# Batch attention of a fused perceiver block: gate and power projections laid between the halves of scores and values, cosine products on VectorE

## The chip, the cores and the metric

The kernel runs on one NeuronCore of one Trainium2 chip. The metric is the device time of one execution in microseconds (us), the median of several runs. Of the core's engines the text names TensorE (PE in the rows, PEld for its weight loads), VectorE (DVE), ScalarE (ACT), GpSimd (POOL) and SyncE (SP), which only issues DMAs here.

## The reference, cut to what matters

The reference is six residual sublayers over x of 32 x 32 tokens by 512. The change lies in the second one. It is an attention over the 32 sequences of each time step's batch, with 16 heads of 32, where keys and queries are scaled by two running quantities, a gate and a power:

```python
q = _l2norm((xn @ Wq).reshape(Bx, Tx, H, Dh))
k = _l2norm((xn @ Wk).reshape(Bx, Tx, H, Dh))
v = (xn @ Wv).reshape(Bx, Tx, H, Dh)
clock = jax.nn.softplus(xn @ clock_w + clock_b).reshape(Bx, Tx, H, 1)
q = _rope(q, times)                      # pairs turned by cos and sin of the token's place
k = _rope(k, times)
gj = -jax.nn.softplus(xn @ gate_w + gate_b).reshape(Bx, Tx, H, Dh)
gcp = jnp.exp(jnp.clip(jnp.cumsum(gj, axis=1), -60.0, 50.0))
q = q * gcp
k = k / (gcp + 1e-08)
p = (xn @ p_w + p_b).reshape(Bx, Tx, H, Dh)
p_max = jnp.max(p, axis=1, keepdims=True)
p_exp = jnp.exp(p - p_max) * clock
p_cs = jnp.cumsum(p_exp, axis=1)
q = q / (p_cs + 1e-08)
k = k * p_exp
scores = jnp.einsum('bqhd,bkhd->bhqk', q, k) / math.sqrt(Dh)
scores = jnp.where(mask[None, None], scores, -jnp.inf)
attn = jax.nn.softmax(scores, axis=-1)
out = jnp.einsum('bhqk,bkhd->bqhd', attn, v).reshape(Bx, Tx, D)
```

The other sublayers (a delayed-aggregation attention before it; a GELU MLP, a mixture of small experts, a cross attention, a state-space scan and a ternary MLP behind it) are not touched.

## The kernel before

All activations are held transposed: 128 features on the partitions, 1024 token columns, four feature groups `o` = 0 to 3 of four heads each. A projection of one group onto one half of the tokens is one **unit**: `project_half` (L506 is its matmul, inside `linear`) multiplies four 128x128 blocks of a weight with four 128x512 blocks of XN into one PSUM bank. All is fp32, and the trace shows each fp32 matmul as two rows, so a unit is 8 rows of L506. The weights are bq, bk (queries, keys), bg (gate), bp (power) and bv (values).

PSUM has eight banks in two rings of four. A bank of the first ring is filled by TensorE and emptied by ScalarE (`open_act`, semaphores act_bank_full and act_bank_free); one of the second is emptied by VectorE (`open_dve`). A ring's bank number u can be opened when number u-4 has been emptied, so the order of the units in a ring must be the same on both engines. Every engine's order is written out by hand; nothing is planned by a program.

For one group o the steps are these. ScalarE takes the gate's projection out of PSUM with its bias (`gate_half`, L1285) and makes log(1+exp) of it with three activations (`gates_in`, L1299 to L1301). It takes out the power's projection (`powers_in`, L1318) and makes two exponentials (`gates_exp`, L1322 and L1324). VectorE does the running sums and the quotient (`gates`, L1854 to L1876, among them a RECIPROCAL of 128x1024 at L1871). TensorE spreads the clock (`clocks`, L630), projects queries and keys, turns them by a matrix (`rotations`, L638) and sums squares (`norm_sums`, L648), while ScalarE copies and squares them (`queries_keys`, L1330, L1196). VectorE multiplies the turned ones by sin (`rotate`, L1882), and GpSimd multiplies the plain ones by cos (L2386); VectorE adds and scales (L1887 to L1890) and makes the norm's inverse (`norm`, L1895, L1896). TensorE spreads it (`norm_spread`, L659), and VectorE multiplies it in (`spread_norm`, L1902). Then `scores` lays the causal mask (L670) and multiplies queries and keys in 128 tiny matmuls of 32x32 (L680, 256 rows), ScalarE takes exp (L1357), `values` multiplies with the values in another 128 tiny matmuls (L694, 256 rows), VectorE divides (`normalise`, L1909, L1910), and `turn` transposes (L704).

The loop over o on TensorE runs: bp of group o+1, clocks(o+1), scores(o), turn(o-1), bq and bk of o+1, rotations(o+1), norm_sums(o+1), bg of group o+2 (for o below 2), values(o), norm_spread(o+1). VectorE's loop is gates(o+1), rotate(o+1), norm(o+1), normalise(o), spread_norm(o+1).

The arena has six slots of 1 MB for weights. `free_after_act` and `free_after_dve` note at which count of a ring's full banks a slot may be loaded again; SyncE waits for that count. Behind the loop the first weight of the MLP goes into the slot of bk and the second into that of bg.

Of the kernel before, what the change touches and what calls it, by code (L numbers as in the profile page):

```python
# [17 lines left out]
C2 = N // 512  # L18
# [76 lines left out]
def perceiver(nc, dram, out):  # L95
# [6 lines left out]
    with ctx:  # L102
# [364 lines left out]
        def _(pe):  # L467
# [195 lines left out]

            def scores(o):

                heads = [open_act(("s", o, h)) for h in range(4)]
                for i in range(4):
                    for h in range(4):
                        hp = slice(32 * h, 32 * h + 32)
                        mm(heads[h][32 * i:32 * i + 32, 0:256].rearrange("p (x n) -> p x n", x=TT), tab("ident")[hp, hp],  # L670
                           tab("causal")[hp, :].unsqueeze(1).to_broadcast([32, TT, 32]), start=True, stop=False,
                           tile_position=(32 * h, 32 * i), skip_group_check=True)
                for tt in range(TT):
                    if tt % 4 == 0:
                        on_dve(("n", o, 1, tt // 4))
                    for i in range(4):
                        tok = slice(128 * tt + 32 * i, 128 * tt + 32 * i + 32)
                        for h in range(4):
                            hp = slice(32 * h, 32 * h + 32)
                            last = mm(heads[h][32 * i:32 * i + 32, 32 * tt:32 * tt + 32], H[hp, 0, 1, tok], H[hp, 0, 0, tok],  # L680
                                      start=False, stop=(tt == TT - 1), tile_position=(32 * h, 32 * i), skip_group_check=True)
                            if tt == TT - 1 and i == 3:
                                last.then_inc(act_bank_full, 1)

            def values(o):
                for u in range(4):
                    on_act(("s", o, 3))
# [33 lines left out]
            for c in range(C2):  # L721
                features(0, c, "plain")
            norm_spread(0)
            for o in range(4):
                if o < 3:
                    project(o + 1, ("bp",))
                    clocks(o + 1)
                scores(o)
                if o:
# [5 lines left out]
                if o < 2:  # L735
                    project(o + 2, ("bg",))
# [3 lines left out]
            for w in ("bq", "bk", "bg", "bp"):  # L740
                free_after_act(w)
            turn(3)
# [443 lines left out]
        def _(act):  # L1186
# [118 lines left out]
            def gates_in(o):  # L1305

                if o:
                    for c in range(C2):
                        gate_half(o, c)
                act.wait_ge(act_bank_free, UA.at[("bg", o, C2 - 1)] + 1)  # L1310
# [35 lines left out]
            for c in range(C2):  # L1346
                features(0, c, Y, "plain")
            for o in range(4):
                if o < 3:
                    powers_in(o + 1)  # L1350
# [11 lines left out]
                if o < 2:  # L1362
                    gates_in(o + 2)
            turned(3)
# [304 lines left out]
        def _(dve):  # L1669
# [179 lines left out]
            def gates(o):  # L1849
# [13 lines left out]
                for c in range(C2):  # L1863
                    b = unit(("ck", o, c))
                    v.tensor_tensor(p[:, ch(c)], b[:, :], p[:, ch(c)], ALU.mult).then_inc(dve_bank_free, 1)
                stored(("ck", o, C2 - 1))
# [11 lines left out]
            def rotate(o):  # L1878
                for w, t_ in (("bq", t0), ("bk", t1)):
                    for c in range(C2):  # L1880
# [3 lines left out]
                                        tab("sin").unsqueeze(1).to_broadcast([128, 16, L]), ALU.mult).then_inc(dve_bank_free, 1)  # L1884
                stored(("rbk", o, C2 - 1))
# [488 lines left out]
        def _(pool):  # L2374
# [6 lines left out]
            for o in range(4):  # L2381
                for i, w in enumerate(("bq", "bk")):
                    pool.wait_ge(act_bank_free, UA.at[(w, o, C2 - 1)] + 1)
                    pool.wait_ge(dve_bank_full, UV.at[("r" + w, o, C2 - 1)] + 1)
                    x3 = H[:, 0, i, :].rearrange("p (b l) -> p b l", l=L)
                    g.tensor_tensor(x3, x3, tab("cos").unsqueeze(1).to_broadcast([128, B, L]), ALU.mult).then_inc(S["b_cos"], 1)  # L2386
# [253 lines left out]
```

## Time and profile before

| what | value |
| --- | --- |
| median of 3 runs | 2265.08 us (2259.3 to 2266.7) |
| the profiled execution, its own time | 2268.11 us |
| its span in the trace | 2266.3 us |
| mean granted TensorE clock | 0.974 of full |
| TensorE busy (matmul) | 2110.3 us, 93% |
| VectorE busy | 1249.2 us, 55% |
| ScalarE busy | 921.0 us, 41% |
| GpSimd busy | 91.3 us, 4% |

Times in the rows are us from the start of the span unless marked ns. A row of the timeline gives the start, the busy time, engine, line, operation, output and input, the shape, how many instructions are merged, and in brackets how long the engine stood idle before and what ended that. "issue" as the ender means that the profile shows nothing that the engine waited for. The granted clock is 1.00 at TensorE's upper level (2.4 GHz) and 0.50 at its lower (1.2 GHz). The batch attention's loop lies between 248 and 430 us.

### The profile page before, as it was taken

The numbers are of one execution on the slowest core, as the hardware profiler recorded it, in microseconds if no ns is written. First come the engines' busy times: TensorE is split into PE (matmuls) and PEld (weight loads), VectorE is DVE, ScalarE is ACT, GpSimd is POOL, SyncE is SP. The second block draws the span as 40 slices with busy tenths as digits, with TensorE's granted clock in tenths as the row PEclk, the third lists the DMA queues.
The fourth block names the chain that finished last, engine by engine and source line by source line (L and its number), as shares of the span: only waits on it lengthen the run. The fifth ranks groups of instructions, "written<-read, shape, count | busy, mean of one in ns | idle before, by whom it ended". The sixth has DMA issues, their size and how long they took to land. (4 is left out here: it accounts for less than half of the span.)

```text
span 2266.3 us, 35893 instructions
## 1 busy us (share of the span) xinstructions
PE 2110.3 (93%) x14950; PEld 1533.4 (68%) x14950; DVE 1249.2 (55%) x2086; ACT 921.0 (41%) x2211; POOL 91.3 (4%) x119
## 2 busy tenths in 40 slices
PE   6999898689999999989998999999999999988899
PEld 5764444468867888844445788778878778774587
DVE  4255466363345888799998310544354443456563
ACT  3224333053424323599996332232232322323432
POOL 0000011000000000100000000000000000000122
PEclk9999988799999999999999999999999999999999
DMA  6120000111210110120002144322121121232000
GB/s 237 34 86 1 1 2 2 39 56 38 75 43 19 38 56 22 54 93 19 1 1 94 42 162 145 103 63 65 43 85 43 55 73 43 67 113 91 1 1 37
DMA packets 84872, 127.01 MB, mean 56 GB/s; under 512 B 6998, under 2 KB 48470, under 8 KB 84248
## 3 DMA queue, kind: packets, MB, share of 16 engines
q1 hardware_dynamic: 84712, 124.73, 16.6%
q8 instruction: 119, 1.95, 0.4%
q14 instruction: 41, 0.34, 0.0%
HBM read 109.77 MB, written 14.94 MB: 55 GB/s over the span
## 5 line engine op out<-in xcount | busy, mean ns | idle before, releaser
L1196 ACT ACTIVATE R<-bank 128x512 f32<-128x512 f32 (+3 forms) x157 | 93.0, 597 | 466.8 <-PE bank L891 335.6
L1426 ACT ACTIVATE R<-R 128x64 f32<-128x64 f32 x1024 | 248.0, 356 | 0.0
L891 PE MATMUL bank<-cth,wmh 128*128 128x512 f32 x512 | 208.0, 406 | 7.1 <-ACT arena L1527 6.9
L891 PE MATMUL bank<-cth,wml 128*128 128x512 f32 x512 | 202.3, 395 | 0.0
L891 PE MATMUL bank<-ctl,wmh 128*128 128x512 f32 x512 | 202.0, 395 | 0.0
L506 PE MATMUL bank<-XN,arena 128*128 128x512 f32 x320 | 153.1, 635 | 0.5 <-ACT R L1357 0.5
L891 PEld LDWEIGHTS bank<-cth,wmh 128*128 128x128 f32 x512 | 96.3, 188 | 35.3 <-issue 16.1
L506 PE MATMUL bank<-Y,arena 128*128 128x512 f32 x256 | 117.6, 605 | 0.0
L506 PEld LDWEIGHTS bank<-XN,arena 128*128 128x128 f32 x320 | 64.0, 205 | 78.6 <-issue 77.8
L2173 DVE COPY Y<-bank 128x512 f32<-128x512 f32 x128 | 79.5, 683 | 61.6 <-PE bank L929 61.5
L891 PEld LDWEIGHTS bank<-cth,wml 128*128 128x128 f32 x512 | 96.2, 188 | 22.1
L891 PEld LDWEIGHTS bank<-ctl,wmh 128*128 128x128 f32 x512 | 96.4, 188 | 20.0
L764 PE MATMUL bank<-hid_high,piece_high 128*128 128x512 f32 x256 | 100.3, 392 | 6.2 <-DVE hid_low L2089 6.2
L1527 ACT ACTIVATE arena<-bank,small 128x289 f32<-128x289 f32 x128 | 62.5, 501 | 99.6 <-PE bank L940 52.4
L764 PE MATMUL bank<-y_high,piece_high 128*128 128x512 f32 x256 | 99.8, 390 | 0.0
L764 PE MATMUL bank<-hid_high,piece_low 128*128 128x512 f32 x256 | 99.7, 390 | 0.0
L764 PE MATMUL bank<-y_high,piece_low 128*128 128x512 f32 x256 | 99.7, 390 | 0.0
L764 PE MATMUL bank<-hid_low,piece_high 128*128 128x512 f32 x256 | 99.7, 390 | 0.0
L764 PE MATMUL bank<-y_low,piece_high 128*128 128x512 f32 x256 | 99.7, 389 | 0.0
L2160 DVE TENSOR_TENSOR ctl<-H,cth 128x2048 fp32r<-128x2048 f32 x15 | 34.4, 2293 | 103.4 <-ACT cth L1502 103.4
L1234 ACT ACTIVATE piece_high<-arena 128x512 fp32r<-128x512 f32 x80 | 48.8, 624 | 102.4 <-PE bank L764 102.1
L506 PEld LDWEIGHTS bank<-Y,arena 128*128 128x128 f32 x256 | 49.5, 195 | 60.3 <-issue 60.0
(418 smaller groups left out, 4429.3 us busy)
## 6 DMA issues: line engine op xcount, KB each, us to landing
H<-in_ctxT SPq DMA_DIRECT2D x30, 512.0 KB, 5.1
arena<-in_L_attn_mlp_w SPq DMA_DIRECT2D x8, 1024.0 KB, 5.2
arena<-spill SPq DMA_DIRECT2D x32, 256.0 KB, 5.4
spill<-R SPq DMA_DIRECT2D x3, 2048.0 KB, 8.3
spill<-XN SPq DMA_DIRECT2D x3, 2048.0 KB, 8.3
arena<-in_L_ffn_Wg SPq DMA_DIRECT2D x4, 1024.0 KB, 7.1
arena<-in_L_ffn_Wu SPq DMA_DIRECT2D x4, 1024.0 KB, 5.2
arena<-in_L_ffn_Wd SPq DMA_DIRECT2D x4, 1024.0 KB, 5.5
```

Of the source, the lines that this page charges most:

```text
L506: last = mm(bank, w[:, k, cols_], x[:, k, xc], start=(k == 0), stop=(k == 3 and not more))
L764: last = mm(b[:, :], w_, x_[:, k, ch(c)], start=(k == 0 and i == 0), stop=(k == 3 and i == 2))
L891: last = mm(b[:, :].rearrange("p (a c) -> p a c", a=2), w_, c_[:, k, :, :], start=(k == 0 and n_ == 0), stop=(k == 3 and n_ == 2))
L1196: fn(dst, src, ACT.Copy).then_inc(act_bank_free, 1)
L1234: fn(piece_high[:, n % PIECES], W(name)[:, :, tl(o)], ACT.Copy).then_inc(S["w_high"], 1)
L1426: last = fn(EE[n % 3][:, a:a + 64], RC["Ey"][:, t, h, :], ACT.Copy, scale=RC["Ex"][:, t, h, 8 * j + x:8 * j + x + 1])
L1527: fn(RDa["p"][:, g, 320 * (bb % 2):320 * (bb % 2) + 289], b[:, 0:289], ACT.Exp, bias=small[:, 16 + x:17 + x], scale=HD1 ** -0.5, accum_out ...
L2160: v.tensor_tensor(ctl[:, :, :, :], ct if pr else ct_first, cth[:, :, :, :].bitcast(f32), ALU.subtract).then_inc(S["d_clo"], 1)
L2173: v.tensor_copy(RD["vt"][:, 2 * (bb % 2) + blk, 512 * half:512 * half + 512], b[:, :]).then_inc(dve_bank_free, 1)
```

## The change

On TensorE the gate's projections of groups 2 and 3 (two units each) leave their place ahead of values(o) and go into the scores of group o: the first unit after half of the tiny matmuls, the second right after the last. They are now written into VectorE's ring of banks. The power's projections of groups 2 and 3 leave the head of the loop and go into values(o), before its third and fourth quarter; group 1's two go ahead of the loop, before norm_spread(0). VectorE takes the gate's projections of groups 2 and 3 out of PSUM, with the bias, in the middle of gates(o+1); ScalarE no longer does. ScalarE's powers_in moves behind gates_in. The products with cos go from GpSimd to VectorE, inside rotate. The slot of bg is released by the count of VectorE's ring.

```diff
--- before.py
+++ after.py
@@ -661,6 +661,10 @@
                             if s_ == 3:
                                 last.then_inc(dve_bank_full, 1)
 
+            def gate_unit(o, c):
+                b = open_dve(("bg", o, c))
+                linear(b[:, :], W("bg"), tl(o), XN, ch(c)).then_inc(dve_bank_full, 1)
+
             def scores(o):
 
                 heads = [open_act(("s", o, h)) for h in range(4)]
@@ -671,6 +675,8 @@
                            tab("causal")[hp, :].unsqueeze(1).to_broadcast([32, TT, 32]), start=True, stop=False,
                            tile_position=(32 * h, 32 * i), skip_group_check=True)
                 for tt in range(TT):
+                    if tt == 4 and o < 2:
+                        gate_unit(o + 2, 0)
                     if tt % 4 == 0:
                         on_dve(("n", o, 1, tt // 4))
                     for i in range(4):
@@ -684,6 +690,8 @@
 
             def values(o):
                 for u in range(4):
+                    if u in (2, 3) and o < 2:
+                        project_half("bp", o + 2, u - 2)
                     on_act(("s", o, 3))
                     b = open_dve(("pv", o, u))
                     for t in range(2):
@@ -720,25 +728,26 @@
             pe.wait_ge(S["n_plain"], TT)
             for c in range(C2):
                 features(0, c, "plain")
+            project(1, ("bp",))
             norm_spread(0)
             for o in range(4):
                 if o < 3:
-                    project(o + 1, ("bp",))
                     clocks(o + 1)
                 scores(o)
+                if o < 2:
+                    gate_unit(o + 2, 1)
                 if o:
                     turn(o - 1)
                 if o < 3:
                     project(o + 1, ("bq", "bk"))
                     rotations(o + 1)
                     norm_sums(o + 1)
-                if o < 2:
-                    project(o + 2, ("bg",))
                 values(o)
                 if o < 3:
                     norm_spread(o + 1)
-            for w in ("bq", "bk", "bg", "bp"):
+            for w in ("bq", "bk", "bp"):
                 free_after_act(w)
+            free_after_dve("bg")
             turn(3)
             weight("bo")
             on_act(("turn", 3, 1))
@@ -1304,10 +1313,13 @@
 
             def gates_in(o):
 
-                if o:
+                if o == 1:
                     for c in range(C2):
                         gate_half(o, c)
-                act.wait_ge(act_bank_free, UA.at[("bg", o, C2 - 1)] + 1)
+                if o < 2:
+                    act.wait_ge(act_bank_free, UA.at[("bg", o, C2 - 1)] + 1)
+                else:
+                    vrow(("bg", o, C2 - 1))
                 if o:
                     act.wait_ge(S["b_gcs"], o)
                 log1pexp(gate_buf[o % 2], RB["lg"][:, 0, :], S["b_gsp"])
@@ -1345,9 +1357,9 @@
             gates_in(1)
             for c in range(C2):
                 features(0, c, Y, "plain")
+            powers_in(1)
             for o in range(4):
                 if o < 3:
-                    powers_in(o + 1)
                     gates_exp(o + 1)
 
 
@@ -1361,6 +1373,7 @@
                     queries_keys(o + 1)
                 if o < 2:
                     gates_in(o + 2)
+                    powers_in(o + 2)
             turned(3)
 
             def inputs(c):
@@ -1863,6 +1876,10 @@
                 for c in range(C2):
                     b = unit(("ck", o, c))
                     v.tensor_tensor(p[:, ch(c)], b[:, :], p[:, ch(c)], ALU.mult).then_inc(dve_bank_free, 1)
+                if 0 < o < 3:
+                    for c in range(C2):
+                        v.tensor_scalar(gate_buf[(o + 1) % 2][:, ch(c)], unit(("bg", o + 1, c))[:, :], col("L0_attn_gate_b", o + 1), None, ALU.add
+                                        ).then_inc(dve_bank_free, 1)
                 stored(("ck", o, C2 - 1))
                 step(v.tensor_tensor_scan(pcs, reset[:, 0, :], p, 0.0, ALU.mult, ALU.add))
                 step(v.tensor_scalar(pcs, pcs, 1e-8, None, ALU.add))
@@ -1876,12 +1893,16 @@
                 step(v.tensor_tensor(rg, g, rg, ALU.mult))
 
             def rotate(o):
-                for w, t_ in (("bq", t0), ("bk", t1)):
+                cos = tab("cos").unsqueeze(1).to_broadcast([128, B, L])
+                for w, t_, x in (("bq", t0, q), ("bk", t1, k)):
                     for c in range(C2):
                         b = unit(("r" + w, o, c))
                         v.tensor_tensor(t_[:, ch(c)].rearrange("p (b l) -> p b l", **byb),
                                         b[:, :].rearrange("p (b l) -> p b l", **byb),
                                         tab("sin").unsqueeze(1).to_broadcast([128, 16, L]), ALU.mult).then_inc(dve_bank_free, 1)
+                    on_act((w, o, C2 - 1))
+                    x3 = x.rearrange("p (b l) -> p b l", **byb)
+                    v.tensor_tensor(x3, x3, cos, ALU.mult).then_inc(S["b_cos"], 1)
                 stored(("rbk", o, C2 - 1))
                 dve.wait_ge(S["b_cos"], 2 * (o + 1))
                 v.tensor_tensor(q, q, t0, ALU.add)
@@ -2378,12 +2399,6 @@
             g.memset(RA["m"], 0.0).then_inc(m_zero, 1)
             pool.wait_ge(in_consts, 32)
             end_stage()
-            for o in range(4):
-                for i, w in enumerate(("bq", "bk")):
-                    pool.wait_ge(act_bank_free, UA.at[(w, o, C2 - 1)] + 1)
-                    pool.wait_ge(dve_bank_full, UV.at[("r" + w, o, C2 - 1)] + 1)
-                    x3 = H[:, 0, i, :].rearrange("p (b l) -> p b l", l=L)
-                    g.tensor_tensor(x3, x3, tab("cos").unsqueeze(1).to_broadcast([128, B, L]), ALU.mult).then_inc(S["b_cos"], 1)
             end_stage()
             end_stage()
             pool.wait_ge(dve_bank_full, UV.at[("cu", NQ - 1, 3, C2 - 1)] + 1)
```

## Rows read from the trace of the kernel before

**Rows 1.** Page: busy time by engine, clock by slice, instruction queue (packets, MB, share)
```profile
PE 2110.3 (93%) x14950; PEld 1533.4 (68%) x14950; DVE 1249.2 (55%) x2086; ACT 921.0 (41%) x2211; POOL 91.3 (4%) x119
PEclk9999988799999999999999999999999999999999
q8 instruction: 119, 1.95, 0.4%
```

**Rows 2.** TensorE's timeline, group 0, from the spread of the norm to its scores
```profile
248.42 1.72 PE L659 MATMUL bank<-H,consts 32*128 32x128 f32 x32
250.07 7.13 PE L506 MATMUL bank<-XN,arena 128*128 128x512 f32 x16
257.13 1.98 PE L630 MATMUL bank<-R,consts 16*128 16x512 f32 x4
259.04 0.72 PE L670 MATMUL bank<-consts 32*32 32x256 f32 x32
...
261.61 1.29 PE L680 MATMUL bank<-H 32*32 32x32 f32 x128 [0.78 <-issue]
265.06 0.36 PE L680 MATMUL bank<-H 32*32 32x32 f32 x16 [2.17 <-issue]
265.90 16.99 PE L506 MATMUL bank<-XN,arena 128*128 128x512 f32 x32 [0.47 <-ACT R L1357]
```

**Rows 3.** TensorE's timeline, from group 0's values to the start of group 3
```profile
294.32 2.55 PE L694 MATMUL bank<-R 32*32 32x33 f32 x256
...
299.03 1.69 PE L659 MATMUL bank<-H,consts 32*128 32x128 f32 x14 [0.67 <-issue]
300.65 9.81 PE L506 MATMUL bank<-XN,arena 128*128 128x512 f32 x16
...
312.30 0.71 PE L670 MATMUL bank<-consts 32*32 32x256 f32 x32
...
352.12 0.56 PE L694 MATMUL bank<-R 32*32 32x33 f32 x40 [2.12 <-issue]
...
366.92 0.71 PE L670 MATMUL bank<-consts 32*32 32x256 f32 x32
...
390.58 3.60 PE L638 MATMUL bank<-H,consts 128*128 128x512 f32 x8
...
404.63 3.22 PE L659 MATMUL bank<-H,consts 32*128 32x128 f32 x32 [4.58 <-DVE R L1910]
```

**Rows 4.** Stretches: length, busy PE, PEld, DVE, ACT, POOL, clock, DMA, GB/s
```profile
252.01:301.76 49.75, 45.67 (x683) 23.61 (x682) 36.78 (x39) 19.09 (x26) 4.66 (x2) 0.91 0.01 2
266.00:268.00 2.00, 2.00 (x3) 0.97 (x4) 1.97 (x2) 0.67 (x3) 0.00 (x0) 0.50 0.04 8
272.00:274.00 2.00, 2.00 (x6) 0.94 (x5) 1.97 (x2) 1.08 (x2) 0.00 (x0) 1.00 0.00 0
299.00:299.50 0.50, 0.47 (x7) 0.47 (x8) 0.29 (x1) 0.50 (x1) 0.00 (x0) 0.75 0.00 0
```

**Rows 5.** Timelines of ScalarE, VectorE and GpSimd, gates and rotation of groups 1 and 2
```profile
260.47 1.06 ACT L1324 ACTIVATE R<-R 128x1024 f32<-128x1024 f32 x1 [0.18 <-DVE R L1860]
267.20 6.55 DVE L1871 RECIPROCAL R<-R 128x1024 f32<-128x1024 f32 x1
284.75 4.66 POOL L2386 TENSOR_TENSOR H<-H,consts 128x1024 f32<-128x1024 f32 x2 [79.29 <-PE bank L638]
289.51 1.23 DVE L1887 TENSOR_TENSOR H<-H,R 128x1024 f32<-128x1024 f32 x1 [2.47 <-POOL H L2386]
311.22 1.22 DVE L1859 TENSOR_REDUCE R<-H 128x32 f32<-128x1024 f32 x1 [5.19 <-ACT H L1318]
```

**Rows 6.** The loop's end: TensorE, SyncE's issues, a stretch (columns of rows 4)
```profile
425.38 0.66 PE L694 MATMUL bank<-R 32*32 32x33 f32 x32 [5.29 <-issue]
415.45 1.64 SPq L2439 DMA_DIRECT2D arena<-in_L_attn_mlp_w  x2
418.00:420.00 2.00, 1.88 (x127) 1.85 (x127) 0.88 (x4) 0.00 (x0) 0.00 (x0) 0.50 1.12 377
```

## The prediction, made before the changed kernel ran

> **What bounds the kernel now.** I read the page first: TensorE is busy 93% of the span, and its granted clock, near full nearly everywhere, dips in slices 5 to 7, that is from 283 to 453 us [rows 1]. The batch attention lies there. Then I read TensorE's timeline through its loop. A group takes 53.3 us at first (mask row at 259.04 to mask row at 312.30) and 54.6 us then (to 366.92) [rows 2, 3], and the reader should see that three things in it are no work.
>
> First, waits with the ender "issue" inside the runs of tiny matmuls: 0.78 and 2.17 us in group 0's scores, 0.67 us behind its values, 2.12 us in group 1's values [rows 2, 3]. A tiny matmul goes by in some 10 ns (128 rows in 1.29 us), and the waits come 128 rows apart [rows 2]. With their weight loads these are 256 instructions, and the instruction queue moved 1.95 MB in 119 packets, 16.4 KB each, 64 bytes for each of 256 instructions [rows 1]. I read the waits as instruction blocks that are used up before the next is there. From the end of one wait (261.61) to the end of the next (265.06) are 3.45 us [rows 2]; I take that as the pace at which blocks come. A unit of a projection is 8 rows and takes 7.13 / 2 = 3.57 us [rows 2]: 16 instructions in which the queue catches up by a whole block.
>
> Second, the clock. At 266 it is at its lower level, where 32 rows of bq and bk take 16.99 us against 2 x 7.13 = 14.3, so 2.7 us are lost; at 272 it is back at the upper [rows 2, 4]. It falls again near 299.2, and bp of group 2 takes 9.81 us against 7.13, again 2.7 lost [rows 3, 4]. Before the first fall TensorE had done nothing full-width since bp and clocks ended at 259.1, before the second nothing since 294.3: only tiny matmuls and waits. Third, 0.47 us of wait for ScalarE's exp [rows 2].
>
> VectorE is not behind: of the 49.75 us between the starts of two gates it is busy 36.78 [rows 4], and it waits for the power's projection (5.19 us in group 2) [rows 5]. Its chain becomes important below.
>
> **TensorE in groups 0 and 1.** No matmul is added or removed. Group 0 without the three losses is 53.3 - (0.78 + 2.17 + 0.67) - 0.47 - 2.7 - 2.7 = 43.8 us. *The waits for instructions.* With a unit after half of the scores' tiny matmuls, another behind them and two between the quarters of values, nearly any 256 instructions in a row contain a unit or the clocks' 1.98 us [rows 2], so the pace of 3.45 us is kept. Between 0 and 2.2 us (one whole wait) may stay for each group, depending on where block ends lie; I take 0. *The wait for exp:* the second gate unit, 3.57 us, lies between the last score and bq, and exp of four banks is over by then; 0 stays.
>
> *The clock.* The values' stretch is cut into pieces below 2.3 us between units, and I drop its fall. But with bp gone from the loop's head, the stretch from values' last unit to the scores' first unit holds only narrow work: last quarter 0.6, norm_spread 1.7, clocks 1.98, mask and half the scores 2.1, and handovers, 6.4 to 7.4 us. The two falls came 4.9 us (294.3 to 299.2) and at most 7 us (259.1 to 266) after the last wide work [rows 2 to 4]. So I keep one fall for each group, which now slows the gate units in the scores. Its price is 0 (none) to 2.7 us; I take 1.8, since part of a low stretch lies on tiny matmuls that are bound otherwise. Group 0 then takes 45.6 us, a gain of 7.7. Group 1 has the same work and one turn, 8 rows of a quarter of a unit's columns, 3.57 / 4 = 0.9 us: 46.5 us, and 54.6 - 46.5 = 8.1.
>
> **VectorE in groups 0 and 1.** It gets two PSUM reads of 128x512 for the gate. No row has this form; half of an L1887 row (1.23 us for 128x1024) is 0.62, a whole one 1.23 [rows 5]; I take 0.7 each, nearer to the row of its width, 1.4 in all (1.2 to 2.5). It gets two cos products with L1887's shape, 2 x 1.23 = 2.5 us. Against that goes its wait for GpSimd, which needed 4.66 us for the pair, 2.47 of it shown as VectorE's wait [rows 5]: on VectorE the first product falls into gaps between the rotations, and the last ends about 0.4 us earlier than GpSimd's. In group 0's own rotation the 2.5 us are hidden by the value projection and by the features behind it. The chain from one gates to the next is 36.78 + 1.4 + 2.5 = 40.7 us, plus 1.1 for ScalarE's exponential of the power [rows 5], plus about 1 for handing the norm to TensorE and back: 42.8 us. The 5.19 us wait goes, since bp is out of PSUM before VectorE asks. So VectorE runs just below TensorE's 43.8 to 46. **The added wait:** VectorE now waits for the second gate unit in the middle of gates. Behind it stand the scan, the RECIPROCAL of 6.55 us [rows 5], rotate and norm, and norm_spread waits for them. I get the unit done 0.4 to 0.8 us after VectorE is ready; that fits in the slack and is not charged.
>
> **Ahead of the loop.** bp of group 1 was behind norm_spread(0) and covered its reading by VectorE; now it stands before. TensorE's sum is the same, scores(0) start some 0.3 us later (bank handovers). VectorE's first gates start 7 us later, at 259, which the chain above contains. Cost 0.3.
>
> **Group 2.** Here the cover is gone: bp and clocks stood ahead of scores(2), now only clocks. VectorE starts gates(3) about when scores(2) start. ScalarE makes the two exponentials of the gate and power first: before, from 252.01 to 260.47 + 1.06, 9.5 us, less 1.7 us of waiting for bp, 7.8 us [rows 4, 5]. Scores take 3.5 us and a wait of about 1.8, so TensorE stands about 2.5 us until exp of the scores frees a bank for turn. Behind it is bq and bk. From the rotations (390.58) to norm_spread (404.63, 4.58 us late) [rows 3] VectorE's chain decides, and it is 0.4 us shorter. Net -2.1 (0 to -5).
>
> **The loop's end.** Two MLP weights of 1 MB each start at 415.45 and fill the DMA engines (share 1.12 at 418 to 420), and TensorE then waits 5.29 us for instructions [rows 6]. bg's slot is now released by VectorE's ring, whose count at that place includes the last values bank. So the second MB starts only when values(3) is over, where wide matmuls follow and the next stage still is far. Other waits of this kind are up to 2.2 us, so the gain lies between 0 and 3.1; I take 2.5. SyncE has nothing else queued behind.
>
> **Sum.** 7.7 + 8.1 - 0.3 - 2.1 + 2.5 = 15.9 us. Against the profiled execution's 2268.11 us that is 2252.2; the median of the runs, 2265.08, lies 3.0 below that execution, so the forecast is 2249.2 us.
>
> **A rule against it.** The rows above show 0.78 + 2.17 + 0.67 + 2.12 = 5.7 us of "issue" in two groups [rows 2, 3] and one packet for each 256 instructions [rows 1]. The Trainium skill, "Runtime: NRT & Kernel Launch", section "Instruction fetch mechanics", has the same 16 KiB blocks, but gives TensorE a store of 128 KiB, eight blocks, and calls the crossing of a block mostly hidden; a run of some 580 instructions could then never wait. By that rule the waits have another cause and would stay: that is the first rival. The waits 128 rows apart speak against it.
>
> **Rivals.** *The waits and falls stay* (the tiny matmuls themselves are the cause). Then only the exp wait (1), the weight's delay (2.5) and VectorE's lost wait for bp count, less 2.4: about 3 to 6 us, 2260.5. For it: I infer the blocks. Against: their regular distance. Chance 0.12. *VectorE becomes the bound:* its reads cost 1.23 us each, and with each late gate unit (a fall stretches the unit to 7 us) the whole chain moves, 3 us more for each group: gain 10, 2255.1. For it: 42.8 stands only 1 us below 43.8. Chance 0.17. *No fall at all:* 2 x 1.8 more, and the first MB hurts less: gain 20.5, 2244.6. For it: every stretch of narrow work gets shorter in total. Chance 0.2. *Slower:* with a unit between runs of tiny matmuls the clock stays down: in the rows it came back within bq and bk, a row of 16.99 us of nothing but wide work [rows 2, 4]. All wide work of groups 0 and 1, about 8 units and the rotations, 32 us each, runs at half speed: each group loses up to 32 us instead of 1.8. It becomes slower than before when the loss is over 15.9 / 2 + 1.8 = 10 us for each group, about 20 us of wide work at the low level; if half of the wide work ran so, 2 x 14 more, 2277. Against it: bq, bk and the rotations are still 18 us in a row. Chance 0.03.
>
> **How the numbers follow.** The forecast's case has 0.48. Its own bounds (a wait of 2.2 left in each group, a fall at 2.7, no gain at the end) reach 2257; the best case reaches 2244.6, and the before runs themselves spread by 7 us. Range 2240 to 2258. A change below 0.3%, 6.8 us, can't be told from none here. Faster: 0.48 + 0.17 + 0.2 and a quarter of the first rival, 0.88; same 0.08; slower 0.04.
>
> **What would show it.** Right: "issue" waits inside L680 and L694 of groups 0 and 1 gone; mask rows 45 to 47 us apart; bq and bk back at 14.3 us; at most one stretch at 0.50 for each group, lying on the gate units; ScalarE's wait for bp gone; one 1 MB load before and one after values(3). Wrong: VectorE's wait at its second gate read above 2 us, norm_spread waiting for L1910 in groups 1 and 2 by more than 2 us, or the waits moved to other rows.

## The result, and the profile after

| | median | runs | range |
| --- | --- | --- | --- |
| before | 2265.4 us | 5 | 2259.3 to 2266.7 |
| changed | 2248.23 us | 5 | 2244.97 to 2251.45 |

The ratio is 0.9924, with a 95% interval of 0.9908 to 0.994. That is 17.2 us faster by the medians; the forecast was 15.9 us, 2249.2. The profiled execution of the changed kernel took 2248.23 us, its span is 2246.2.

TensorE's timeline of group 0 and the start of group 1 (start, busy time, instruction, and in brackets the idle time before and what ended it) answers [rows 2] and the start of [rows 3]. L674, L686 and L702 are now the mask, the scores and the values:

```profile
255.38 1.72 PE L659 MATMUL bank<-H,consts 32*128 32x128 f32 x32
257.40 1.95 PE L630 MATMUL bank<-R,consts 16*128 16x512 f32 x4 [0.31 <-DVE H L1923]
259.28 0.71 PE L674 MATMUL bank<-consts 32*32 32x256 f32 x32
259.74 1.33 PE L686 MATMUL bank<-H 32*32 32x32 f32 x112
261.52 0.29 PE L686 MATMUL bank<-H 32*32 32x32 f32 x16 [0.44 <-issue]
261.74 3.70 PE L506 MATMUL bank<-XN,arena 128*128 128x512 f32 x8
265.37 1.29 PE L686 MATMUL bank<-H 32*32 32x32 f32 x128
266.59 17.43 PE L506 MATMUL bank<-XN,arena 128*128 128x512 f32 x40
...
288.40 1.35 PE L702 MATMUL bank<-R 32*32 32x33 f32 x128
289.68 3.70 PE L506 MATMUL bank<-XN,arena 128*128 128x512 f32 x8
...
302.77 1.15 PE L674 MATMUL bank<-consts 32*32 32x256 f32 x32
```

The reader is to see three things. Of the waits for instructions, 0.78 and 2.17 us in the scores and 0.67 us behind the values, 0.44 us in the scores is left. A unit of 8 rows stands behind 128 tiny rows. And the 40 rows from 266.59 (the second gate unit, bq and bk) take 17.43 us, where 32 rows took 16.99 before [rows 2]: the clock is at its upper level. Group 0 takes 43.5 us (259.28 to 302.77), where it took 53.3.

Group 1's scores, first before and then changed:

```profile
314.90 1.27 PE L680 MATMUL bank<-H 32*32 32x32 f32 x128 [1.24 <-issue]
318.63 0.91 PE L680 MATMUL bank<-H 32*32 32x32 f32 x67 [2.46 <-issue]
```

```profile
303.62 1.77 PE L686 MATMUL bank<-H 32*32 32x32 f32 x128
305.32 4.12 PE L506 MATMUL bank<-XN,arena 128*128 128x512 f32 x8
```

The prediction counted 5.7 us of "issue" in the two groups; with these two waits, which it left out, they are 9.4 us. All 5.8 us of group 1's are gone. Group 1 takes 44.3 us (302.77 to 347.11), where it took 54.6.

From group 2 on, the same view answers the end of [rows 3] and the first row of [rows 6]:

```profile
347.11 1.16 PE L674 MATMUL bank<-consts 32*32 32x256 f32 x32
...
350.67 1.53 PE L686 MATMUL bank<-H 32*32 32x32 f32 x127 [0.96 <-issue]
354.94 2.08 PE L712 MATMUL bank<-consts,R 128*128 128x128 f32 x8 [2.74 <-ACT R L1369]
356.81 15.89 PE L506 MATMUL bank<-XN,arena 128*128 128x512 f32 x32
...
385.96 3.22 PE L659 MATMUL bank<-H,consts 32*128 32x128 f32 x32 [3.75 <-DVE R L1931]
...
394.42 0.32 PE L686 MATMUL bank<-H 32*32 32x32 f32 x22 [1.81 <-issue]
...
404.13 0.67 PE L702 MATMUL bank<-R 32*32 32x33 f32 x32 [3.96 <-issue]
...
408.29 17.11 PE L506 MATMUL bank<-R,arena 128*128 128x512 f32 x35 [0.73 <-issue]
```

The 2.74 us ahead of turn are the new wait for exp that the missing cover gives. The last wait for instructions fell from 5.29 to 3.96 us. The first bo row starts at 408.29 instead of 429.54.

VectorE's timeline of group 1 and a stretch of all engines (length, busy PE, PEld, DVE, ACT, POOL, clock, DMA share, GB/s) answer [rows 4, 5]:

```profile
267.94 0.74 DVE L1881 TENSOR_SCALAR H<-bank,cols 128x512 f32<-128x512 f32 x1
270.33 0.75 DVE L1881 TENSOR_SCALAR H<-bank,cols 128x512 f32<-128x512 f32 x1 [1.64 <-PE bank L506]
...
288.00 1.21 DVE L1905 TENSOR_TENSOR H<-H,consts 128x1024 f32<-128x1024 f32 x1
```

```profile
258.97:302.45 43.48, 42.53 (x685) 22.03 (x684) 39.86 (x42) 17.44 (x24) 0.00 (x0) 1.00 0.01 2
302.00:304.00 2.00, 2.00 (x50) 0.77 (x52) 1.97 (x3) 0.00 (x0) 0.00 (x0) 0.70 0.00 0
304.00:306.00 2.00, 2.00 (x128) 1.75 (x126) 1.99 (x1) 0.00 (x0) 0.00 (x0) 0.50 0.04 8
306.00:308.00 2.00, 2.00 (x6) 0.77 (x5) 1.94 (x3) 1.06 (x1) 0.00 (x0) 0.95 0.00 0
```

Between the starts of two gates VectorE is now busy 39.86 of 43.48 us, TensorE 42.53: both are nearly full. The gate's read costs 0.74 us, the cos product 1.21. The second read waits 1.64 us for its unit. In this execution group 0 has no low stretch of the clock at all; one lies between 302 and 306, on clocks, mask and scores of group 1.

Since whole executions of one kernel differ by 7 us and more, the experiments are read by stretches of the loop as well: the group lengths are from mask row to mask row, the end from norm_spread(3) to the first bo row, the loop from group 0's mask row to the first bo row. Each line of the table is from one profile, also that of before, whose execution was 2.7 us above its median (2268.1 against 2265.4); the gain is that of the medians, against the runs of before on the same chip.

| kernel | group 0 | group 1 | mask(2) to norm_spread(3) | end | loop | median | gain |
| --- | --- | --- | --- | --- | --- | --- | --- |
| before | 53.3 | 54.6 | 37.7 | 24.9 | 170.5 | 2265.4 | |
| changed | 43.5 | 44.3 | 38.9 | 22.3 | 149.0 | 2248.2 | 17.2 |
| e1 nothing laid between | 50.2 | 52.7 | 38.0 | 23.2 | 164.2 | 2261.5 | 4.9 |
| e2 scores whole | 47.8 | 48.3 | 37.8 | 23.0 | 156.8 | 2254.0 | 12.4 |
| e3 values whole | 48.1 | 49.8 | 36.5 | 22.8 | 157.2 | 2258.6 | 7.8 |
| e4 cos on GpSimd | 45.0 | 43.5 | 39.0 | 22.8 | 150.3 | 2246.4 | 19.9 |
| e5 both loads early | 45.0 | 44.4 | 37.8 | 25.2 | 152.4 | 2252.0 | 15.6 |
| e6 both loads late | 45.4 | 43.6 | 38.2 | 20.8 | 148.0 | 2251.2 | 16.4 |
| e7 e6 and exp first | 47.3 | 44.3 | 36.8 | 21.1 | 149.5 | 2251.6 | 16.0 |
| e8 filler | 45.2 | 45.1 | 37.6 | 24.4 | 152.2 | 2252.0 | 15.6 |
| e9 changed, again | 47.0 | 44.5 | 39.0 | 23.0 | 153.4 | 2247.6 | 19.2 |
| e10 combined | 45.0 | 44.3 | 39.3 | 21.7 | 150.3 | 2249.4 | 17.4 |

### The profile page after: what moved, and what is told of

The parts are those of the page before. It is cut to its first block and busy times, and to the rows that moved or that the text cites. A ratio compares the mean times of both kernels' runs of the same rounds, so it can differ in the third digit from the quotient of the medians.

```text
span 2246.2 us, 35885 instructions
## 1 busy us (share of the span) xinstructions
PE 2102.9 (94%) x14950; PEld 1528.6 (68%) x14950; DVE 1258.8 (56%) x2098; ACT 917.9 (41%) x2207; POOL 72.6 (3%) x111
## 3 DMA queue, kind: packets, MB, share of 16 engines
q8 instruction: 119, 1.95, 0.4%
## 5 line engine op out<-in xcount | busy, mean ns | idle before, releaser
L506 PE MATMUL bank<-XN,arena 128*128 128x512 f32 x320 | 146.4, 610 | 0.0
L900 PEld LDWEIGHTS bank<-cth,wml 128*128 128x128 f32 x512 | 96.2, 188 | 22.3
L900 PEld LDWEIGHTS bank<-ctl,wmh 128*128 128x128 f32 x512 | 96.5, 188 | 20.1
L1243 ACT ACTIVATE piece_high<-arena 128x512 fp32r<-128x512 f32 x80 | 48.8, 624 | 102.9 <-PE bank L773 102.7
```

The costliest lines, as they stand in the source:

```text
L506: last = mm(bank, w[:, k, cols_], x[:, k, xc], start=(k == 0), stop=(k == 3 and not more))
L900: last = mm(b[:, :].rearrange("p (a c) -> p a c", a=2), w_, c_[:, k, :, :], start=(k == 0 and n_ == 0), stop=(k == 3 and n_ == 2))
L1243: fn(piece_high[:, n % PIECES], W(name)[:, :, tl(o)], ACT.Copy).then_inc(S["w_high"], 1)
```

## The experiments

### e1: the same order, nothing laid between

```diff
-                    if tt == 4 and o < 2:
-                        gate_unit(o + 2, 0)
...
-                    if u in (2, 3) and o < 2:
-                        project_half("bp", o + 2, u - 2)
...
                 scores(o)
                 if o < 2:
+                    gate_unit(o + 2, 0)
                     gate_unit(o + 2, 1)
...
+                if o < 2:
+                    project(o + 2, ("bp",))
                 values(o)
```

> The changed kernel with its four gate units behind the whole scores and its four power units ahead of the whole values, so no unit lies between tiny matmuls; all else as changed (the power of group 1 ahead of the loop, gate read and cos on VectorE, late weight slot). If the laying between pays (blocks of instructions arrive every 3.45 us and the clock holds when wide work comes between), the waits for instructions come back: about 2 to 3.5 us in each of the scores of groups 0 and 1, 0.7 to 2 us in each of their values, and each group shows a low clock on the units behind; groups 0 and 1 take some 50 us instead of 43.5 and 44.3, and the kernel is 9 to 13 us slower than the changed one, about 2259. If the gain came from the order alone (VectorE's wait for the power's projection gone), they stay at 43.5 to 45 us and the time at 2248 to 2250.

Measured: 2261.49 us, ratio to before 0.9982 (0.9967 to 0.9996); groups 0 and 1 take 50.2 and 52.7 us. TensorE's timeline of group 1 and the end of group 0 in e1:

```profile
305.73 1.60 PE L659 MATMUL bank<-H,consts 32*128 32x128 f32 x29 [0.90 <-issue]
...
316.36 0.77 PE L684 MATMUL bank<-H 32*32 32x32 f32 x67 [2.19 <-issue]
317.06 8.83 PE L506 MATMUL bank<-XN,arena 128*128 128x512 f32 x16
...
356.14 0.99 PE L698 MATMUL bank<-R 32*32 32x33 f32 x56 [2.13 <-issue]
```

The waits are back, 2.2 us in scores and 2.1 in values, and two gate units take 8.83 instead of 7.13 us: a low clock. All the rest of the change gives 6.3 us of the loop (170.5 less 164.2); the laying between gives 15.2 by the changed kernel's first profile (149.0), 10.8 by its second (153.4, e9), and 12.3 by the medians (17.2 less 4.9). The expectation held in kind. The time, told as 9 to 13 us over the changed kernel and about 2259, came out 13.3 over it and at 2261.5.

### e2 and e3: one of the two laid between

e2 is the scores' part of e1's edit alone, e3 the values' part alone:

```diff
e2:
-                    if tt == 4 and o < 2:
-                        gate_unit(o + 2, 0)
...
                 if o < 2:
+                    gate_unit(o + 2, 0)
                     gate_unit(o + 2, 1)
e3:
-                    if u in (2, 3) and o < 2:
-                        project_half("bp", o + 2, u - 2)
...
+                if o < 2:
+                    project(o + 2, ("bp",))
                 values(o)
```

> The changed kernel with only the gate units taken out of the scores and put behind them. If block supply bounds the tiny matmuls: waits of 1.5 to 3.5 us in the scores of each of groups 0 and 1, then a low clock on the gate units; groups 0 and 1 each 3 to 5 us longer, kernel 2254 to 2258. The second gate unit then ends that much later, and VectorE's wait at its second read grows by the same amount from the 1.64 and 2.16 us it has. If the waits are due to something else, nothing appears and the time stays near 2248.

> The changed kernel with only the power units taken out of the values and put ahead of them. The values then run as 256 rows on end: a wait of 0.7 to 2.1 us for instructions in each of groups 0 and 1 and a longer narrow stretch to the scores of the next group (values, norm_spread, clocks, half the scores: some 8 to 9 us), on which the clock falls in both groups; 1.5 to 4 us more for each group, kernel 2251 to 2256. If VectorE's chain decides the group's length, the waits hide behind its norm and only the clock's part shows: under 2 us in all.

e2: 2253.95 us, 0.9954 (0.9936 to 0.9972); the loop is 7.8 us longer than the changed kernel's. e3: 2258.59 us, 0.9966 (0.9953 to 0.9979); 8.2 us longer. These are against the first profile. Groups 0 and 1 together took 87.8 to 91.6 us, mean 89.7, in the eight profiles that have them as changed (e9 below); e2 takes 96.1 (6.4 more), e3 97.9 (8.2 more), e1 102.9 (13.3 more). The two sum to 14.6, so the parts are near additive. From e2, group 1's scores, then from e3, group 1's values and what follows:

```profile
310.69 0.91 PE L684 MATMUL bank<-H 32*32 32x32 f32 x67 [2.00 <-issue]
311.53 8.75 PE L506 MATMUL bank<-XN,arena 128*128 128x512 f32 x16
```

```profile
347.70 0.84 PE L700 MATMUL bank<-R 32*32 32x33 f32 x56 [1.90 <-issue]
348.48 3.10 PE L659 MATMUL bank<-H,consts 32*128 32x128 f32 x32
351.42 3.75 PE L630 MATMUL bank<-R,consts 16*128 16x512 f32 x4
```

In e2 a wait of 2.00 us and 1.6 us of low clock on the two units behind. In e3 a wait of 1.90 us, then norm_spread and clocks at half speed: 3.10 and 3.75 us against 2.09 and 1.95. The expectation for e2 held (groups 4.3 and 4.0 us longer, 2254); VectorE's wait for the gate grew as told, but at both reads: 3.13 and 2.68 us in group 0, where the changed kernel's profile has none and 1.64. The one for e3 missed: 2258.6 us against 2251 to 2256, groups 4.6 and 5.5 us longer against 1.5 to 4. My bound for e3, that VectorE's chain might hide it, falls. By the gains (12.4 and 7.8 us) e3 is the dearer of the two, but their intervals overlap. Waits for instructions make 2.7 us of e3's 8.2 in groups 0 and 1 (0.83 and 1.90); most of the rest is narrow work at the lower clock, as in the rows above. In group 2 e3 wins 2.4 us back: TensorE waits 0.89 us for exp and 0.70 for instructions at turn instead of 2.74 for exp, and bq and bk take 14.53 us instead of 15.89; its wait for VectorE's side ahead of norm_spread(3) is no shorter (4.22 against 3.75).

### e8: a unit in scores(3) that computes nothing needed

```diff
+                    if tt == 4 and o == 3:
+                        b = open_dve("filler")
+                        linear(b[:, :], W("bp"), tl(0), XN, ch(0)).then_inc(dve_bank_full, 1)
...
+                if o == 2:
+                    v.tensor_copy(small[:, 40:48], unit("filler")[:, 0:8]).then_inc(dve_bank_free, 1)
```

> The changed kernel with one more unit, whose product is thrown away, after half of the tiny matmuls of scores(3). If blocks of instructions come every 3.45 us, the unit's 3.57 us give the time for the next: the 1.81 us wait in those scores goes wholly, and the price of the added unit (3.5 us at the upper level, up to 7 at the lower) is partly paid: net 1.7 to 5 us slower. If the wait belongs to the tiny matmuls, it stays at 1.8 and the kernel is 3.5 us or more slower.

TensorE's timeline through the scores of group 3 in e8 (L689 are the scores, L715 is turn):

```profile
388.28 1.16 PE L674 MATMUL bank<-consts 32*32 32x256 f32 x32
389.13 1.76 PE L689 MATMUL bank<-H 32*32 32x32 f32 x128
390.82 4.67 PE L506 MATMUL bank<-XN,arena 128*128 128x512 f32 x8
395.42 1.29 PE L689 MATMUL bank<-H 32*32 32x32 f32 x128
397.23 1.06 PE L715 MATMUL bank<-consts,R 128*128 128x128 f32 x8 [0.52 <-ACT R L1372]
```

The wait of 1.81 us in these scores is gone. Nothing else in them changed, so it was no property of the tiny matmuls: it goes when 4.67 us of other work stand in their middle. From mask to turn it takes 8.95 us against 6.22 (389.11 to 395.33 in the changed kernel) and 6.58 (e9), so a unit of 4.67 us costs 2.4 to 2.7 there, and 1.4 to 2.1 over the whole end (24.4 us against 22.3 and 23.0), around the low end of the 1.7 to 5 expected. The median, 2252.02 us (0.9927, 0.991 to 0.9944), can't tell that from the changed kernel.

### e5 and e6: when the MLP's weights are loaded

e5 releases bg's slot by ScalarE's ring again; e6 releases bk's slot by VectorE's too:

```diff
e5:
-            for w in ("bq", "bk", "bp"):
+            for w in ("bq", "bk", "bg", "bp"):
                 free_after_act(w)
-            free_after_dve("bg")
e6:
-            for w in ("bq", "bk", "bp"):
+            for w in ("bq", "bp"):
                 free_after_act(w)
-            free_after_dve("bg")
+            for w in ("bk", "bg"):
+                free_after_dve(w)
```

> The changed kernel with the slot of bg released by ScalarE's ring again, so that both 1 MB weights start together as before the change. My step for the loop's end: the second MB in front of TensorE's instruction block makes its last wait in values(3) about as long as before, 5.3 us, instead of the 3.96 us that it has now: 1.3 to 2.5 us slower, norm_spread(3) to the first bo row 23.6 to 24.9 us instead of 22.3. Rival: the wait is set by the first MB alone; then it stays near 4 us and nothing changes.

> The changed kernel with the slot of bk released by VectorE's ring too, so both weights start only when values(3) is over. If the DMAs in front of the instruction block make part of the 3.96 us wait, it falls to the 1.8 to 2.2 us that the other waits have, and the kernel gets 1.8 to 2.2 us faster, about 2246; the weights still arrive more than 20 us before the next stage. If the wait is no matter of the DMA queue, it stays 3.96 us and the time with it.

The last wait in values(3), e5 and then e6:

```profile
408.67 0.67 PE L702 MATMUL bank<-R 32*32 32x33 f32 x32 [5.58 <-issue]
```

```profile
404.81 0.67 PE L702 MATMUL bank<-R 32*32 32x33 f32 x32 [1.45 <-issue]
```

With 2 MB in front the wait is 5.58 us (5.29 before). With 1 MB it is 3.96, and 2.82 to 4.32 in the seven profiles that have this. With none it is 1.45 in e6 and e7, 2.60 in e10. The end takes 25.2, 22.3 and 20.8 us in e5, changed and e6. The instruction queue's own packets separate the cases better: the packet ahead of this wait started behind the one before it by 7.3 and 7.4 us with 2 MB, 5.2 to 5.8 with 1 MB, 3.4 to 4.0 with none. So the second MB adds 2 us; the rival, that the first MB alone sets the wait, is out.

The waits moved the way both expectations told, e6's further (1.45 us against 1.8 to 2.2). e5's end lies just over the 23.6 to 24.9 us told, and e6's time does not come out at 2246. The medians, 2252.03 (0.9931, 0.9915 to 0.9948) and 2251.18 us (0.9928, 0.991 to 0.9947), don't separate these few us; only the stretch shows them.

### e4: cos on GpSimd

```diff
-                    on_act((w, o, C2 - 1))
-                    x3 = x.rearrange("p (b l) -> p b l", **byb)
-                    v.tensor_tensor(x3, x3, cos, ALU.mult).then_inc(S["b_cos"], 1)
...
+            for o in range(4):
+                for i, w in enumerate(("bq", "bk")):
+                    pool.wait_ge(act_bank_free, UA.at[(w, o, C2 - 1)] + 1)
+                    pool.wait_ge(dve_bank_full, UV.at[("r" + w, o, C2 - 1)] + 1)
+                    x3 = H[:, 0, i, :].rearrange("p (b l) -> p b l", l=L)
+                    g.tensor_tensor(x3, x3, tab("cos").unsqueeze(1).to_broadcast([128, B, L]), ALU.mult).then_inc(S["b_cos"], 1)
```

> The changed kernel with the two cos products of each group back on GpSimd. My working: VectorE loses 2.4 us of work for each group but waits about 2.5 us for GpSimd's 4.66 us pair, which can start only when the last rotation is in. In groups 0 and 1 VectorE comes to the rotations late (at 286.8, the rotations done at 287.4), so GpSimd's pair, 287.5 to 292.2, lies in the open: VectorE's add starts at about 292.2 instead of 291.65, norm_spread some 0.5 us later in each group, and 0.4 us later in group 2; together 1 to 2 us slower, which a median can hardly tell. Rival: VectorE is the bound and its 2.4 us count fully: 2 us faster for each of groups 0 and 1, 4 to 5 us in all.

VectorE and GpSimd in e4, group 1's rotation:

```profile
286.84 2.48 DVE L1899 TENSOR_TENSOR R<-bank,consts 128x512 f32<-128x512 f32 x4
291.45 1.23 DVE L1904 TENSOR_TENSOR H<-H,R 128x1024 f32<-128x1024 f32 x1 [2.12 <-POOL H L2403]
```

```profile
285.92 5.42 POOL L2403 TENSOR_TENSOR H<-H,consts 128x1024 f32<-128x1024 f32 x2 [82.96 <-PE bank L638]
```

VectorE's add starts 4.61 us behind the start of its sin products, and in the changed kernel 4.86 (286.79 to 291.65). So in groups 0 and 1 moving cos to VectorE neither gains nor loses: 2.4 us of work replace 2.1 us of waiting. GpSimd begins with queries as soon as their rotation is in, which I had overlooked, and ends earlier than I said. 2246.41 us, 0.9925 (0.9899 to 0.9951). The 1 to 2 us slower and the rival's 4 to 5 us faster both lie within what the medians leave open; in the stretches neither is there (groups 0 and 1 take 88.5 us, of 87.8 to 91.6 in the eight).

### e9, e7 and e10: how far one profile can be trusted, and a try at more

e9 is the changed kernel, unchanged. e7 is e6 with the exps of scores(2) ahead of the power's exponential. e10 is e7 with turn(1) ahead of clocks(3):

```diff
                 fn(gate_buf[o % 2], RB["t"][:, 1, :], ACT.Exp).then_inc(S["b_gcp"], 1)
+                if o == 3:
+                    score_exps(2)
                 act.wait_ge(S["b_pdif"], o + 1)
...
+                if o == 2:
+                    turn(1)
                 if o < 3:
                     clocks(o + 1)
                 scores(o)
...
-                if o:
+                if o in (1, 3):
                     turn(o - 1)
```

> The changed kernel itself once more, on the same chip as the next one. In five runs above, all with groups 0 and 1 ordered as here, group 0 took 45.0 to 47.3 us where the changed kernel's profile has 43.5, each with a low stretch of the clock on the first gate unit (4.9 to 5.5 us instead of 3.7). If that profile was a lucky one, this one shows such a stretch in group 0 and 45 us or more; if the changed kernel is free of it by its own order, 43.5 us again. Time 2246 to 2252.

> The last one, and in group 2 ScalarE makes the four exps of the scores before the exponential of the power. TensorE's 2.74 us wait for them ahead of turn(1) falls to about 0.5 us; the power's exponential comes at most 0.3 us later, so VectorE, which had 2.0 us to spare at the rotations of group 3, becomes about level with TensorE. Group 2 up to norm_spread(3) gets 1.5 to 2.2 us shorter: 2244. If VectorE's chain already set group 2's end, under 0.5 us.

> The changed kernel with both MLP weights loaded behind values(3), the exps of scores(2) ahead of the power's exponential on ScalarE, and turn(1) ahead of clocks(3) instead of behind scores(2). Turn no longer stands between the scores' end and bq, and TensorE waits about 0.5 us there instead of 2.7: from the mask row of group 2 to its bq row 5.5 to 6.5 us instead of 9.7, then VectorE's chain (2.0 us to spare) takes back about half. Loop's end 1.5 us shorter as in the run with both loads late. In all 2.5 to 4.5 us faster than the changed kernel, 2244 to 2246. If VectorE's chain takes all back in group 2, only the 1.5 us of the end are left, which the median can't tell.

e9: 2247.6 us, 0.9917 (0.9894 to 0.9941). Its group 0:

```profile
263.51 5.61 PE L506 MATMUL bank<-XN,arena 128*128 128x512 f32 x8
```

The same unit took 3.70 us in the first profile. Group 0 takes 47.0 us, and clocks of group 1 stretch too. So the first profile was the lucky one: in all eight profiles with this order of groups 0 and 1 (changed, e4 to e10), group 0 takes 43.5 to 47.3 us, mean 45.4, and group 1 43.5 to 45.1, mean 44.3. Only the first profile has no low stretch in group 0; in group 1 there is none in four of the eight (e4, e5, e6, e10).

e7: 2251.63 us, 0.9926 (0.9902 to 0.9951). The expected 2244 was missed. Its stretch of group 2 is 36.8 us against 38.2 in e6, 1.4 less, where 1.5 to 2.2 was told: the wait for exp ahead of turn fell from 2.34 us to 0.52 as told, but a wait of 1.24 for instructions came up inside turn. e10: 2249.37 us, 0.9929 (0.9907 to 0.9951), not the expected 2244 to 2246, and its group 2 got no shorter, 39.3 us. TensorE and VectorE there:

```profile
353.21 1.34 PE L686 MATMUL bank<-H 32*32 32x32 f32 x128 [2.01 <-issue]
356.94 0.33 PE L686 MATMUL bank<-H 32*32 32x32 f32 x7 [2.39 <-issue]
357.67 15.68 PE L506 MATMUL bank<-XN,arena 128*128 128x512 f32 x32 [0.40 <-ACT R L1338]
```

```profile
359.41 1.29 DVE L1889 TENSOR_TENSOR R<-bank,R 128x512 f32<-128x512 f32 x2 [4.78 <-ACT R L1346]
```

With turn moved, the ends of instruction blocks fall otherwise: the scores meet two waits, 2.01 and 2.39 us, and the last seven rows hang on the second. ScalarE, whose power exponential now stands behind these scores, holds VectorE 4.78 us. My expectation had counted neither. In e10 both MLP weights load late too, and still its last wait in values(3) is 2.60 us where e6 and e7 have 1.45; there the values ran 224 rows on end without the shorter wait (0.31 and 0.59 us) that e6 and e7 have between. Neither of the two beats the changed kernel by its time.

## Why the prediction was right

**The bound and the waits for instructions.** Right, and shown. e1 to e3 bring the waits back, e8 takes away another, e5 and e6 stretch and shrink one by what is loaded ahead of it. That they are waits for blocks of instructions, which the prediction inferred from their distance, can be read from the trace directly. Two stretches of before, around the end of group 0's first 240 score rows (a wait from 262.9 to 265.06):

```profile
262.50:263.00 0.50, 0.40 (x46) 0.28 (x32) 0.47 (x2) 0.00 (x0) 0.00 (x0) 1.00 0.13 33
263.00:265.00 2.00, 0.00 (x0) 0.00 (x0) 2.00 (x1) 0.00 (x0) 0.00 (x0) 1.00 0.00 0
```

The 33 GB/s of the first row are one packet of the instruction queue. Its record runs from 262.71 to 263.72, and the wait ends 1.3 us later. It is so everywhere: in the loop of all twelve profiles, each of the 81 waits marked "issue", other than the last one before bo, ended 1.2 to 1.6 us after such a packet was through. The 0.73 us before bo is of another kind: in eleven of twelve profiles no packet stands in the 5 us before its end. The rule of the Trainium skill that the prediction set against them ("Runtime: NRT & Kernel Launch", section "Instruction fetch mechanics": a store of eight blocks, crossings mostly hidden) does not agree with e8 and e6, where the wait went from 1.81 to 0 and from 3.96 to 1.45 us; the measurement decides. I took 0 left per group: 0.44 in group 0 and 0 in group 1 were left in the first profile, and at most 1.02 in a group (e5, group 1) in the eight.

**The clock.** I kept one fall for each group at 1.8 us and so got 45.6 and 46.5 us. Over eight profiles the means are 45.4 and 44.3. Group 0's term holds: seven of the eight have a fall, which begins on clocks ahead of the mask row, and its first gate unit then takes 5.07 to 5.61 us, 1.4 to 1.9 over its 3.70. Group 1's term is the mis-sized one, by 2.2 us. Four of the eight have no fall there, and they take 43.5 to 44.4 us; the four with one take 44.3 to 45.1, their gate unit 4.10 to 4.92 us. So a fall in group 1 costs well below 1.8, and the group is also some 0.7 us shorter without one than the 44.7 that my terms give (43.8 and 0.9 for turn).

The sign that I went by, the length of the stretch without wide work, does not decide it. In the first profile the clock stayed at its upper level through 6.4 us of norm_spread, clocks, mask and scores (255.38 to 261.74); in seven others the same stretch brought a fall. The prediction also counts clocks once as wide (last wide work to 259.1) and once as narrow.

**Ahead of the loop.** Forecast 0.3. From TensorE's first row behind L526 (the last work ahead of bp and norm_spread) to the first mask row it takes 10.6 us before and 10.9 in the first profile, 0.3 more; in the other seven, where the low clock reaches into clocks, it takes 11.4 to 11.6, 0.8 to 1.0 more. So the term holds only without the fall.

**VectorE.** The gate's read costs 0.74 and 0.75 us (0.7 taken), cos 1.21 (1.23 taken). Its busy time per group is 39.86 (40.7 taken). The wait at the second read was put at 0.4 to 0.8 and is 1.64 and 2.16 us, and 3.8 to 4.0 in group 0 of the seven profiles with a fall on the gate unit. I had written that more than 2 us there would show me wrong. That sign was met, and it was the wrong sign: this wait is time in which VectorE has nothing to do, and what counts is whether norm_spread then waits for VectorE. It waits 0.27 to 0.53 us in group 0 and not at all in group 1, in all eight, far below the 2 us of my second sign. So VectorE is not the bound, but the two engines do run within some 3 us of each other.

**Group 2.** The mechanism is as told: a wait of 2.74 us for exp (2.5 told), bq and bk at 15.89 (a low clock behind it). Net it cost 1.1 us (38.9 against 37.7), and 0.7 by the mean of the six profiles with this order of group 2 (38.4); I said 2.1.

**The loop's end.** 24.9 us became 22.3, so 2.6 against 2.5, and 2.2 by the mean of changed, e4 and e9 (22.7). e5 gives it back (25.2). Right and shown. It comes from both waits in values(3), 5.29 to 3.96 and 1.19 to 0.16 us; I had only the first. The second is 0.31 us in e5 too, so it is no matter of the loads.

**Sum.** By these means 7.9 + 10.3 - 0.8 - 0.7 + 2.2 = 18.9 us, against 15.9 forecast, 17.2 by the medians of the first five runs and 19.2 by e9's. The 3.0 us between are group 1 (2.2) and group 2 (1.4), less 0.6 net for the other three terms. So part of the nearness of 17.2 to 15.9 is luck: the terms err in both directions, and the gain itself differs by 2 us between two sets of runs of one kernel. The changed kernel's own profile has 21.2 us less at the first bo row (429.54 to 408.29), but its span is only 20.1 us shorter: 1.1 us differ behind the loop, where nothing changed. What that is stays open. The forecast's own bounds add up to 2257.9 us, not 2257.

**The rivals.** "Waits and falls stay" put 2260.5 us on a kernel whose waits and falls all stay; e1, with the same other changes and nothing laid between, took 2261.5. "No fall at all" is what the first profile shows in group 0 and four of the eight show in group 1; no profile shows it in both. "Slower" failed: the clock came back on units that stood alone between tiny matmuls, as at 306 to 308 above.

## What to carry to other kernels

In this kernel runs of tiny matmuls used up their instructions faster than new blocks came, and a few wide matmuls from elsewhere, laid every 128 rows, took nearly all of these waits away and some of the clock's falls. They cost little but their own time: 1.4 to 2.7 us net for a unit of 4.67 us that did no needed work (e8). Look what the moved work had covered where it came from: here a wait of 2.74 us appeared in the group that had nothing more to lay in. Keep large loads from starting while a run of tiny matmuls waits for its instructions; 1 MB in front put the next packet of instructions off by some 2 us, 2 MB by nearly 4. And take several profiles of one kernel before reading a term of 1 or 2 us from one of them.

## What the runs showed of the hardware

**The clock can fall while TensorE is busy.** Stretches of e4, from clocks on to the first gate unit (columns as above):

```profile
256.00:257.00 1.00, 1.00 (x3) 0.18 (x1) 1.00 (x3) 0.00 (x0) 0.00 (x0) 0.85 0.00 0
257.00:258.00 1.00, 1.00 (x22) 0.30 (x33) 1.00 (x1) 0.00 (x0) 0.00 (x0) 0.50 0.08 16
258.00:260.00 2.00, 2.00 (x160) 1.69 (x128) 1.97 (x2) 0.00 (x0) 0.00 (x0) 0.50 0.00 0
262.00:264.00 2.00, 2.00 (x4) 0.81 (x3) 1.46 (x2) 0.67 (x2) 0.00 (x0) 0.62 0.00 0
```

Each of these rows (260 to 262 is left out and alike) shows TensorE without a gap, and yet it is at the lower level from 257 on. What it did before: a wide unit until 253.3, norm_spread (matmuls of 32 of the array's rows), 0.31 us of wait until 255.27, then clocks (16 rows). It is back within the wide gate unit, which starts at 260.08. So no long wait is needed for a fall. Narrow work alone does not decide it either: in the changed kernel's first profile the same order of work kept the upper level, and before, at 263 to 265 above, the clock was at 1.00 while TensorE stood idle.

**The place of a fall shifts between two executions of one kernel.** The same unit took 3.70 and 5.61 us, the loop 149.0 and 153.4 us.

**Instruction blocks can be late, and loads make them later.** A packet of 16.4 KB of the instruction queue was through 1.2 to 1.6 us before each of the 81 waits ended. In values(3) the next packet started 3.4 to 4.0 us after the last with no load in front, 5.2 to 5.8 with 1 MB and 7.3 to 7.4 with 2 MB.
